# Attention b: weighted values in 64x64 quadrants, in two parts around the next scores, and a new order of ScalarE's and VectorE's work inside a step

## The reference

```python
# attention b: x is (8, 256, 128), 16 heads of 64
K = jnp.einsum('bpd,ihd->biph', x, W_K)
Q = jnp.einsum('bpd,ihd->biph', x, W_Q)
V = jnp.einsum('bpd,ihd->biph', x, W_V)
scores = jnp.einsum('biph,biqh->biqp', K, Q)
scores = jnp.where(tril_mask[None, None, :, :], scores, NEG_INF)
attn = jax.nn.softmax(scores / np.sqrt(d_head), axis=-1)
z = jnp.einsum('biph,biqp->biqh', V, attn)
out = jnp.einsum('bqf,df->bqd', z_flat, W_O)
# FFN: every token goes to the expert with the largest affinity x @ centroids.T
```

## Time and profile before

| | us |
|---|---|
| median of 3 runs | 528.8 (528.21 to 530.34) |
| profiled execution | 524.73 |
| its span | 522.9 |

### The profile page before, as it was taken

The page is one execution under the profiler, slowest core; times in us unless marked ns, Lnnn a source line. Parts: engine busy times, 40 slices in busy tenths (PEclk is TensorE's granted clock), DMA queues, the critical chain, the costliest instruction groups (busy, mean ns, idle before and its releaser), DMA issues.

```text
span 522.9 us, 11650 instructions
## 1 busy us (share of the span) xinstructions
PE 433.8 (83%) x3882; PEld 340.7 (65%) x3882; DVE 370.5 (71%) x1466; ACT 253.6 (49%) x867; POOL 239.0 (46%) x250
## 2 busy tenths in 40 slices
PE   2857896634999289999999999999999998439993
PEld 1324555523999246787777778777776787339992
DVE  6699998961666358857779687796879776456661
ACT  1641000512444037758757678576774857115450
POOL 6100988471455224544435345463445546314453
PEclk9987999555999689999999999999999999859997
DMA  8999930034673200000000000000000000136640
GB/s 310 359 389 422 419 158 1 22 106 118 213 207 116 85 2 2 1 1 3 1 1 4 1 1 13 11 21 3 1 11 12 22 1 22 42 101 203 195 140 6
DMA packets 22234, 48.98 MB, mean 94 GB/s; under 512 B 3328, under 2 KB 13574, under 8 KB 19744
## 3 DMA queue, kind: packets, MB, share of 16 engines
q1 hardware_dynamic: 18880, 40.86, 22.3%
q0 software_dynamic: 3296, 7.39, 4.5%
HBM read 24.99 MB, written 24.15 MB: 94 GB/s over the span
## 4 chain that ended last, share of the span: by engine, by line
PE 62%; DVE 17%; issue 6%; ACT 5%; POOL 5%; DMA 3%; POOLq 0%; SPq 0%; DVEq 0%; ACTq 0%
PE ps L868 9%; PE ps L881 8%; PE ps L924 8%; PE ps L999 6%; PE ps L1012 6%; PE ps L966 5%; PE ps L941 4%; PE ps L931 4%; ACT vT L657 3%; PE ps L758 3%; POOL vT L520 2%; PE ps L776 2%; PE ps L716 2%; POOL sorted_in L490 2%; DVE prod L1110 2%
## 5 line engine op out<-in xcount | busy, mean ns | idle before, releaser
L520 POOL TENSOR_TENSOR vT<-vT,prec 128x256 f32<-128x256 f32 (+1 forms) x128 | 103.1, 826 | 129.5 <-DVE prec L1446 128.7
L657 ACT ACTIVATE vT<-vT,nmax 128x128 f32<-128x128 f32 (+1 forms) x256 | 113.4, 448 | 14.3 <-DVE nmax L1436 14.1
L1436 DVE CUSTOM_DVE_ANT_0 vT<-ps,cst 128x128 f32<-128x128 f32 (+1 forms) x256 | 77.5, 350 | 5.4 <-PE ps L966 5.3
L665 ACT COPY prod<-ps 128x384 f32<-128x384 f32 x96 | 42.9, 482 | 60.6 <-PE ps L999 60.6
L924 PE MATMUL ps<-xnT,wb 128*128 128x256 f32 x256 | 68.0, 389 | 1.4 <-DVE qk L1417 0.9
L999 PEld LDWEIGHTS ps<-cst,vT 128*128 128x128 f32 x384 | 42.7, 141 | 30.7 <-POOL vT L520 15.3
L999 PE MATMUL ps<-cst,vT 128*128 128x128 f32 x384 | 54.5, 278 | 4.1 <-POOL vT L520 3.1
L1417 DVE COPY qk<-ps 128x512 f32<-128x512 f32 x64 | 43.4, 678 | 13.6 <-PE ps L924 13.5
L881 PE MATMUL ps<-w2s,pv 128*128 (+1 forms) x368 | 49.3, 277 | 0.8 <-issue 0.8
L924 PEld LDWEIGHTS ps<-xnT,wb 128*128 128x128 f32 x256 | 44.8, 195 | 7.6 <-DVE qk L1417 2.4
L657 ACT ACTIVATION_READ_ACCUMULATOR vT<-vT,nmax 128x1 f32 x256 | 49.0, 191 | 0.0
(11 more groups left out here) (150 smaller groups left out, 794.6 us busy)
## 6 DMA issues: line engine op xcount, KB each, us to landing
sorted_in<-zero SPq DMA_DIRECT2D x1, 16512.0 KB, 64.8
pv<-in_w SPq DMA_DIRECT2D x30, 259.0 KB, 4.0
pv<-sorted_in SPq DMA_DIRECT2D x46, 129.0 KB, 2.8
wps<-in_w SPq DMA_DIRECT2D x1, 2072.0 KB, 9.4
w2s<-in_w SPq DMA_DIRECT2D x1, 2048.0 KB, 14.1
wb<-in_w_b SPq DMA_DIRECT2D x1, 1536.0 KB, 22.9
xres<-in_x SPq DMA_DIRECT2D x4, 256.0 KB, 3.9
xres<-in_bo_a POOLq DMA_DIRECT2D x2, 512.0 KB, 13.8
```

The costliest lines, as they stand in the source:

```text
L520: last = nc.gpsimd.tensor_tensor(px, px, view(prec, m_at(n, x) + t * 2, [[1, 2], [0, (t + 1) * P]]), ALU.mult)
L657: last = nc.scalar.activation(px, px, ACT.Exp, bias=nmax[:, m:m + 1], scale=-1.0, accum_out=psum[:, m:m + 1])
L1436: ins = nc.vector.tensor_tensor_reduce(out=pb[:, o:o + w], in0=wide[:, c:c + w], in1=cst[:, mask:mask + w], scale=-1.0, scalar=-MASKED * 2 ...
```

## The change

The weighted values are multiplied in 64x64 quadrants. The array's rows are then half of a block of 128 keys, and of the queries only those from that key half on are streamed. A group's values are made in two parts: part 0 takes x = 0 from the first 64 rows and x = 1 from the last 64, part 1 the other way round. So the two row halves never write the same PSUM bank at once: x = 0 goes to bank 6, x = 1 to bank 7. Part 0 stands at the end of step n, part 1 in step n + 1, between the scores of x = 0 and those of x = 1. The keys are stored in the order 0, 1, 3, 2 of their 64-blocks, as the queries were; a query block 2 then takes two matmuls for its keys.

On DVE the maxima of head 0, the copy of z, the maxima of head 1, an inversion, the maxima of x = 1 and the copy of q and k follow each other; the FFN's pieces stand behind the second inversion and ahead of `copy_p` (means and spread from step 24 on at the end as before). On ACT the exponentials of x = 0 stand around the first two copies, ahead of the copy of v. PSUM places move: q and k of x = 0 go to bank 6 and of x = 1 to bank 3, the turned probabilities of hh = 1 and the next input to bank 4, affinities and ranks to banks 0 and 1, on PE in mid step.

```diff
+PLACES = QUERIES[0] + QUERIES[1]
+KEYS = (((0, 1),), ((0, 2),), ((0, 2), (3, 4)), ((0, 4),))
+AMID = 24
...
+    k = HALF * np.array(PLACES)[k // HALF] + k % HALF
...
+        turn_ps = (bank[0], jb)
+        later = wide[:, 3 * 512:4 * 512]
...
             def step(b, j):
                 n, n1 = (b, j), at(b, j + 1)
                 bv = b + j // 2
+                if ok(n1):
+                    exp_b(n1, 0, [0])
                 if ok(n):
                     copy_p(n, 0, 1)
                     copy_p(n, 0, 0)
                 if ok(n1):
-                    exp_b(n1, 0, [0])
+                    exp_b(n1, 0, [1])
                 if some(bv) and j != 1 or some(b) and j == 1:
                     copy_v(n, (j + 2) % STEPS)
                 if ok(n):
                     copy_p(n, 1, 1)
                 if ok(n1):
-                    exp_b(n1, 0, [1])
                     exp_b(n1, 1)
...
-            def values_b(n):
-                pe.wait_ge(b_pa, 3 * nth(n) + 3)
-                pe.wait_ge(b_pd, nth(n) + 1)
-                pe.wait_ge(b_v, least(nth(n) + 3, NB * STEPS))
-                need(pe, b_z, nth(n))
-                for x in range(2):
-                    for kt in range(T):
+            def values_b(n, part):
+
+                if part == 0:
+                    pe.wait_ge(b_pa, 3 * nth(n) + 3)
+                    pe.wait_ge(b_pd, nth(n) + 1)
+                    pe.wait_ge(b_v, least(nth(n) + 3, NB * STEPS))
+                    if ok(at(n[0], n[1] + 2)):
+                        pe.wait_ge(b_qk, 2 * nth(n) + 5)
+                    need(pe, b_z, nth(n))
+                else:
+                    pe.wait_ge(b_ph, nth(n) + 1)
+                for kt in range(T):
+                    for r in range(2):
+                        x, k, rows = r ^ part, QUERIES[kt][r], slice(r * HALF, (r + 1) * HALF)
                         for hh in range(2):
-                            c = (2 * x + hh) * BLOCKS * P + kt * 2 * P
+                            c = (2 * x + hh) * BLOCKS * P + kt * 2 * P + k % 2 * HALF
                             v = (kt * HB + 2 * (2 * n[1] + x) + hh) * DHB
-                            last = nc.tensor.matmul(bank[2][hh * DHB:(hh + 1) * DHB, x * L + kt * P:(x + 1) * L],
-                                                    vb[:, v:v + DHB], pT[:, c:c + L - kt * P], start=kt == 0,
-                                                    stop=kt == T - 1, skip_group_check=True)
-                last.then_inc(b_pv, 1)
+                            last = nc.tensor.matmul((bank[1], bank[2])[x][hh * DHB:(hh + 1) * DHB, k * HALF:L],
+                                                    vb[rows, v:v + DHB], pT[rows, c:c + L - k * HALF],
+                                                    start=kt == 0 and part == 0, stop=kt == T - 1 and part == 1,
+                                                    skip_group_check=True)
+                last.then_inc((b_ph, b_pv)[part], 1)
 
             def step(b, j):
                 n, n1, n2 = (b, j), at(b, j + 1), at(b, j + 2)
                 bv = b + j // 2
                 if ok(n1):
                     scores_b(n1, 0)
+                if ok(at(b, j - 1)):
+                    values_b(at(b, j - 1), 1)
+                if ok(n1):
                     scores_b(n1, 1)
                 if ok(n):
                     turn_p(n, 0)
                 if ok(n2):
                     project_qk(n2, 0)
...
+            def step(b, j):
+                n, n1, n2 = (b, j), at(b, j + 1), at(b, j + 2)
+                bv = b + j // 2
+                if ok(n1):
+                    scored(n1, 0)
+                    for t in range(T):
+                        max_b(n1, 0, 0, t)
+                if ok(at(b, j - 1)):
+                    copy_z(at(b, j - 1))
+                if ok(n1):
+                    for t in range(T):
+                        max_b(n1, 0, 1, t)
+                if ok(n):
+                    invert(n, 1)
+                if ok(n1):
+                    scored(n1, 1)
+                    for hh in range(2):
+                        for t in range(T):
+                            max_b(n1, 1, hh, t)
+                if ok(n2):
+                    copy_qk(n2, 0)
+                if ok(n1):
+                    invert(n1, 0)
+                g = due("powers", at(b, j - 1))
+                if g is not None:
+                    norm(1, g)
+                g = due("affinity", n)
+                if g is not None:
+                    choose(1, g)
+                if nth(n) != LAST:
+                    g = due("count", n)
+                    if g is not None:
+                        count(1, g)
+                    g = due("rank", n)
+                    if g is not None:
+                        place(1, g)
+                    if nth(n) < AMID:
+                        prepared(n)
+                if n in ((-1, 3), (0, 0), (0, 1)):
+                    statistics_b(nth(n) + 2)
+                if ok(n):
+                    copy_p(n)
+                if ok(n2):
+                    copy_qk(n2, 1)
+                if j == 1 and some(b + 1):
+                    copy_xT(b + 1)
+                if j == 0 and some(b - 1):
+                    residual_b(b - 1)
+                if j == 0 and some(b) and some(b + 1):
+                    norm_b(b + 1)
+                if nth(n) == LAST:
+                    count(1, due("count", n))
+                    place(1, due("rank", n))
+                elif nth(n) >= AMID:
+                    prepared(n)
```

More of the change, by code:

```diff
@@ L604, in turned_v @@
                 n = GROUPS[k][g][1]
-                nc.scalar.copy(vTt[:, 0:n * P], bank[k][:, 0:n * P]).then_inc(f_vTs, 1)
+                nc.scalar.copy(vTt[:, 0:n * P], turn_ps[k][:, 0:n * P]).then_inc(f_vTs, 1)
             def exps(k, g):
@@ L664, in copy_p @@
                 c = (2 * x + hh) * BLOCKS * P
-                nc.scalar.copy(pT[:, c:c + BLOCKS * P], bank[hh][:, 0:BLOCKS * P]).then_inc(b_pa, 1)
+                nc.scalar.copy(pT[:, c:c + BLOCKS * P], turn_ps[hh][:, 0:BLOCKS * P]).then_inc(b_pa, 1)
             def copy_v(n, i):
@@ L914, in turn_xb @@
                 for t in range(T):
-                    last = nc.tensor.transpose(bank[1][:, t * P:(t + 1) * P], xn[:, t * D:(t + 1) * D], ident)
+                    to = jb[:, 0:P] if t == 0 else view(wide, 4 * 512 + P + HALF, late)
+                    last = nc.tensor.transpose(to, xn[:, t * D:(t + 1) * D], ident)
                 last.then_inc(b_xT, 1)
             def project_qk(n, x):
-                need(pe, b_qk, 2 * nth(n) + x)
+                if x == 0:
+                    if nth(n) > 2:
+                        pe.wait_ge(b_z, nth(n) - 2)
+                    else:
+                        need(pe, b_qk, 2 * nth(n) - 1)
+                else:
+                    need(pe, b_mx, 2 * nth(n))
+                    need(pe, b_qk, 2 * nth(n))
                 if n[1] == 0:
@@ L923, in project_qk @@
                     c = i * HB * DHB + (2 * n[1] + x) * P
-                    last = nc.tensor.matmul(jb[:, i * L:(i + 1) * L], wb[:, c:c + P], xnT[:, 0:L], start=True, stop=True)
+                    last = nc.tensor.matmul((bank[1], later)[x][:, i * L:(i + 1) * L], wb[:, c:c + P], xnT[:, 0:L],
+                                            start=True, stop=True)
                 last.then_inc(b_j, 1)
@@ L1026, in step @@
                     project_qk(n2, 0)
+                g = due("affinity", n)
+                if g is not None and nth(n) != LAST:
+                    pe.wait_ge(b_mx, 2 * nth(n) + 3)
+                    affinity(1, g)
+                g = due("rank", n)
+                if g is not None and nth(n) != LAST:
+                    pe.wait_ge(b_mx, 2 * nth(n) + 3)
+                    rank(1, g)
                 if some(bv) and j != 1 or some(b) and j == 1:
@@ L1416, in copy_qk @@
                 dve.wait_ge(b_j, 2 * nth(n) + x + 1)
-                nc.vector.tensor_copy(qk[:, r:r + 2 * L], jb).then_inc(b_qk, 1)
+                nc.vector.tensor_copy(qk[:, r:r + 2 * L], (bank[1], later)[x]).then_inc(b_qk, 1)
             def copy_z(n):
```

126 lines of the change are left out of this document (40 added, 86 removed).

## The result

| | before | after |
|---|---|---|
| median of runs | 528.61 us (528.21 to 530.34, 4 runs) | 553.34 us (549.69 to 554.68, 4 runs) |
| profiled execution's span | 522.9 us | 552.9 us |

The changed kernel is slower: the ratio is 1.0445, with a 95% interval of 1.0401 to 1.0490. The profiled executions lie 30.0 us apart, the medians 24.7: the one of before (524.73) lies under all four runs of the table, the one of the change (554.68) is the slowest of its four.

What follows compares the result with a forecast made beforehand. The prediction took PE as today's bound and three chains through DVE, ACT and POOL after; plain steps +0.5, turnings +0.3, pieces 4.2 + 3.6 + 5.2 + 0.5 made +14.3 us, from 528.8 to 543, range 527 to 554.

Steps and rivals of the forecast that it cites:

- likeliest case: Whole kernel: chains hold the plain step and pieces lengthen theirs, 534 to 551 us; chance 0.60.
- rival 3: Values on PE: the quadrants' row halves serialise, 0.85 or more a part, +0.3 a step, 552 us or more; chance 0.10.
- plain step: A step of attention b without FFN pieces: 6.8 us where it was 6.75, in bounds 6.7 to 7.0.
- chain one: Maxima and copy of z on DVE, then ACT's exponentials and last copy, ahead of the values: next scores at 6.8 us.
- chain three: Head 1's exponentials, DVE's reciprocal, then its copy of probabilities ahead of the values: first values part at 6.1 us.
- chain two: DVE's reciprocal of the second pair, POOL's product, second turn and projection on PE: first values part at 6.1 us.
- Rival 1: PE stays the bound in attention b: 6.4 us a step, pieces as cheap as now, 519 us; chance 0.17.
- The pieces: FFN work on DVE between reciprocal and copy of probabilities: 6.6 us a group, +4.2 in steps 9 to 15, +3.6 in 17 to 23.
- the slack: Room in chain three, 0.1 to 0.15 us, by which a piece lengthens its step less than its own length.
- Steps 24 to 29: Last stretch of attention b, means and spread still at the step's end: 9.0 against 3.4, of which +5.2 us taken.
- Steps -1 to 1: Start of attention b; the forecast's term was for steps 0, 1 and 30, statistics and a norm ahead of the copy: +0.5 us.
- rival 2: FFN pieces on DVE fall into waits and cost as now: about 531 us; chance 0.13.

Runs made afterwards that it cites:

- e3: The changed kernel with ScalarE's order of before (last copy of probabilities ahead of head 1's exponentials): 599.25 us, ratio 1.1314 to the kernel before.
- e4: As e3, with DVE's reciprocal of the first pair moved behind the copy of turned probabilities: 528.05 us, ratio 0.9994 to the kernel before.
- g1: The changed kernel with its own ScalarE order and both DVE reciprocals moved as in f1: 529.64 us, ratio 1.0005 to the kernel before.
- f1: As e4, with DVE's reciprocal of the second pair also moved, right behind the copy of z: 519.38 us, ratio 0.9869 to the kernel before.
- e2: The changed kernel with the values multiplied on 128 rows and 64 columns again, pair by pair: 562.70 us, ratio 1.0645 to the kernel before.
- f3: As f1, with the second values part right behind the first, not between the next scores: 537.85 us, ratio 1.0216 to the kernel before.

## Why the prediction was right

**The number: inside the range, but only just.** The forecast was +14.3 us, the medians say +24.7. 553.34 is 0.7 under the upper end of the range, 554, and above 551, where the prediction's likeliest case ended; the rest of the range was kept for rival 3, which did not happen. Direction, chains and the place of the loss were foreseen; that the number fell inside the range is partly luck.

**What bounds a plain step: right, to 0.03 us.** The forecast was 6.8, the trace has 6.77. Each link of chain one up to ACT's last copy was within 0.03 of the trace; the values then started at 6.17 and not 6.23, and took 0.60 and not 0.56. Each of the three chains was shown by taking others away: e3 leaves chain three as the longest, e4 chain two, g1 chain one, and with none left (f1) PE's own work of 6.44 shows, forecast at about 6.4. One sign came out otherwise: PE was to stand idle 0.3 to 0.4 ahead of the values, but it stood 0.27 ahead of the second turn and 0.04 ahead of the values. Chain two was as long as chain one.

**The quadrants: right.** They run four at a time and save PE 0.3 a step where PE is the bound (f1). Rival 3, part by part 0.85 or more, is out by the 0.55 of a part. Rival 1, PE as the bound at 519 us, did not happen in the change, but its number was right for the kernel in which the chains are gone: f1 measured 519.4.

**The pieces: the mechanism right, the size too small.** The prediction took 6.6 us for a group of pieces, between 5.6 and 8.4. In steps 9 to 15 they cost 9.9 (60.97 less seven steps of 6.77 and 3.7), in steps 17 to 23 10.1. Two things were mis-sized. First, the stalls of small operations came in full. `spread` took 1.71 and `norm` 2.54, more than the 1.43 and 2.36 of before, as the windows of DVE alone show; `means` took 1.29, `choose` 1.74, `count` 0.71 and `place` 1.00. Together that is 9.0, as before, where the prediction reckoned with 7.2 (6.6 and six times 0.1).

```profile
284.52:286.23 1.71, 1.61 (x5) 1.00 0.02 5
299.64:302.18 2.54, 2.50 (x9) 1.00 0.00 0
```

A piece lengthened its step by its own length less about 0.14, the slack that the prediction had put at 0.1 to 0.15: `spread` step 10 by 1.57, `choose` step 13 by 1.59. So the term came to 8.2 without the clock, near its upper bound, 8.4. Second, the prediction had nothing for the clock. After PE's idle time in steps 12 and 20 the output projection ran in part at the lower clock, 5.42 and 5.43 for 3.7. The prediction also took PE's own turning to fit beside the wait; in steps 12 and 20 it waited for `norm` itself, though hardly longer than the copy of probabilities would have held the projection.

Steps 24 to 29 took 5.5 more for a forecast of +5.2, but because errors cancel: over a plain step, steps 25, 26, 27 and 29 took 2.0, 2.5, 2.9 and 1.4 more, where the prediction had 2.6, 1.9, 1.8 and 2.4, and step 27 has the lower clock in it. Steps -1 to 1 took 1.4 more for a forecast of +0.5, step 0 alone 2.1; that was not taken apart.

**The sum.** Steps of attention b: +21.4 us, forecast +14.3. Of the 7.1 that lack, 6.4 are the two stretches with a full group of pieces, about half of it the clock. The profiled executions differ by 8.6 us more outside these steps, 4.7 ahead of them and 3.9 behind. A second execution of the kernel before had 1.7 of the first; the medians put the whole at 24.7, so 3.3 us are left outside the steps. Whether the change causes any of that was not settled: the instructions there are the same but for the last step's, and the lower clock falls differently from trace to trace (PEclk between 0 and 45 us is 0.89 in the trace of before and 0.96 in that of the change).

**"The pieces find cover" (rival 2) is out for the change,** and e4 and g1 show the condition under which it holds: the reciprocal behind the copy.

## What to carry to other kernels

A faster stretch on the busiest engine gives nothing until the chains through the other engines are shorter than what is left of it; add them up link by link from one step's rows, since they may all lie within 0.15 us of each other. On an engine whose instructions run in the order written, a cheap instruction that waits can be the dear one: two reciprocals of 0.18 us each, in the wrong place among copies, maxima and independent pieces, cost this kernel 24 us. A wait of the weight loads is not the same as lost time of the array; compare the starts of the matmuls with a run in which nothing waits. Whether side work belongs mid step or at the end can't be read from one placement; it depends on whether it stands ahead of or behind such a wait.

## What the runs showed of the hardware

- Four 64x64 quadrants with different moving lengths (256 and 64 columns in one row half, 192 and 128 in the other) kept to the sum of columns: a second part took 0.55 to the next instruction, where 320 columns in two records are 0.54. A first part, behind a matmul of another form, took 0.59 (f1).
- Passing from 64x64 values to 64x64 scores cost nothing that shows; from 128x64 to 64x64 and back it cost about 0.15 each time (e2 and f2). The Trainium skill (TensorEngine Tiling (Array Packing), Key Properties) says that a change of tiling mode drains TensorE. The trace agrees: the four parts took 2.38 in f1 and 3.03 in e2, and only 0.22 of the difference is columns.
- In steps 12, 20 and 27 of the changed kernel PE stood idle 1.92, 1.93 and 1.96 us, and shortly after it was granted the lower clock for part of its work: the output projection took 5.42 and 5.43 us for 3.7. It is 16 matmuls in 32 records; the 32 matmuls named ahead of the prediction are records. After 1.56 idle in step 10 the clock stayed at 1.00. What decides it, no run here shows.
- A part that waits for the end of the matmuls just ahead of it on PE starts 0.3 later than one that doesn't (f3).
